# First block's residual halves in the flush of the last attention turn, second stage's weight splits between the first units

## The reference, cut to what matters

```
amp = sigmoid(x @ amp_w + amp_b)
ph = tanh(x @ ph_w + ph_b) * pi
h = (cos(ph) + sin(ph)) * amp
for l in range(2):
    e = h @ ent_w[l] + ent_b[l]
    ent = e @ ent_pw[l] + ent_pb[l]
    h = layer_norm(h + ent, ln3_g[l], ln3_b[l])
    t = einsum('bsd,pdf->pbsf', h, path_w[l]) + path_b[l]
    mod = cos(phase[l]) + sin(phase[l])
    interf = sum(t * mod, over p)
    h = layer_norm(h + interf, ln4_g[l], ln4_b[l])
x = layernorm(x + h)
```

## Time and profile before

| | |
|---|---|
| median of 3 timed runs | 918.68 us (916.01 to 918.86) |
| the profiled execution's own time | 914.03 us |
| its span in the profile | 912.2 us |
| TensorE busy | 858.6 us, 94% |
| VectorE, ScalarE, GpSimd busy | 677.0, 547.0, 491.7 us |
| mean granted clock of TensorE | 0.99 of full |

### The profile page before, as it was taken

How to read it: one execution, slowest core, us unless ns; L and a number is a source line. 1 busy time by engine, 2 the same in 40 slices (tenths; PEclk the granted TensorE clock), 3 DMA queues, 4 the chain that set the end, 5 groups by cost and what they waited for, 6 DMA issues and landing times.

```text
span 912.2 us, 19433 instructions
## 1 busy us (share of the span) xinstructions
PE 858.6 (94%) x5812; PEld 715.1 (78%) x5812; DVE 677.0 (74%) x2061; ACT 547.0 (60%) x1665; POOL 491.7 (54%) x792
## 2 busy tenths in 40 slices
PE   5899999999898999999999999898999999999993
PEld 5778888888787788888888887777778778877773
DVE  4688888888886977777887877758874675666556
ACT  5665556655774666565856566656745645564563
POOL 5456654664665745554645431227760781583387
PEclk9999999999999999999999999999999999999997
DMA  5654434434484956584664638624002002001001
GB/s 183 212 186 148 136 135 168 155 129 152 160 230 139 270 160 199 162 261 115 197 177 154 192 100 266 213 104 162 1 24 70 1 1 92 1 1 45 2 1 47
DMA packets 78939, 117.49 MB, mean 129 GB/s; under 512 B 7888, under 2 KB 41736, under 8 KB 78216
## 3 DMA queue, kind: packets, MB, share of 16 engines
q1 hardware_dynamic: 75416, 112.81, 39.4%
q10 hardware_dynamic: 3440, 3.67, 1.3%
HBM read 58.25 MB, written 17.31 MB: 83 GB/s over the span
## 4 chain that ended last, share of the span: by engine, by line
PE 58%; DVE 6%; SPq 2%; issue 2%; POOL 2%; DMA 2%; ACT 1%; POOLq 0%; DVEq 0%; ACTq 0%
PE bank L161 44%; PE bank L1473 4%; PE bank L1998 3%; PE bank L1496 2%; PE bank L1459 2%; SPq L691 1%; PE bank L1500 1%; DVE stats L1900 1%; DMA xres<-in_x 1%; DVE w_ffn L1685 1%; ACT prob L1079 1%; POOL hT L1793 1%; PE bank L1408 1%; DMA fd<-raw 1%; DVE y L1914 1%
## 5 line engine op out<-in xcount | busy, mean ns | idle before, releaser
L1079 ACT ACTIVATE prob<-bank,nmax 128x128 f32<-128x128 f32 (+1 forms) x512 | 209.2, 432 | 32.8 <-DVE nmax L1224 30.1
L161 PE MATMUL bank<-w_ffn,hT 128*128 128x512 f32 x768 | 188.5, 396 | 1.1 <-DVE w_ffn L1685 0.9
L1224 DVE CUSTOM_DVE_ANT_0 bank<-bank,mask 128x128 f32<-128x128 f32 (+1 forms) x512 | 167.7, 384 | 3.0 <-DVE cv L1172 2.3
L161 PEld LDWEIGHTS bank<-w_ffn,hT 128*128 128x128 f32 x768 | 140.3, 188 | 29.8 <-POOL hT L1793 1.3
L903 POOL TENSOR_TENSOR zone<-raw,zone 128x256 fp32r<-128x256 f32 x128 | 96.2, 783 | 59.7 <-ACT zone L1034 59.7
L1473 PE MATMUL bank<-ident,prob 128*128 128x128 f32 x768 | 119.0, 278 | 1.2 <-ACT probT L1092 1.0
L1092 ACT ACTIVATE probT<-bank 128x512 f32<-128x512 f32 x97 | 58.4, 603 | 95.6 <-PE bank L1500 95.5
L161 PE MATMUL bank<-xT,w_q 128*128 128x256 f32 x768 | 101.9, 284 | 10.5 <-DVE o L1245 9.4
L1079 ACT ACTIVATION_READ_ACCUMULATOR prob<-bank,nmax 128x1 f32 x512 | 111.2, 217 | 0.0
L161 PEld LDWEIGHTS bank<-xT,w_q 128*128 128x128 f32 x768 | 97.8, 190 | 16.0 <-issue 6.0
L161 PE MATMUL bank<-zone 128*128 128x512 f32 x384 | 101.0, 400 | 3.5 <-DVE xT L1147 3.3
(11 more groups left out here) (131 smaller groups left out, 1512.4 us busy)
## 6 DMA issues: line engine op xcount, KB each, us to landing
q<-stage SPq DMA_DIRECT2D x192, 128.0 KB, 2.5
k<-kstage SPq DMA_DIRECT2D x48, 256.0 KB, 4.2
x<-xres SPq DMA_DIRECT2D x16, 512.0 KB, 4.6
raw<-in_ent_wT SPq DMA_DIRECT2D x32, 256.0 KB, 4.1
raw<-in_ent_pw SPq DMA_DIRECT2D x32, 256.0 KB, 4.5
raw<-in_path_w SPq DMA_DIRECT2D x8, 512.0 KB, 3.5
xres<-in_x SPq DMA_DIRECT2D x8, 512.0 KB, 3.8
x1b<-x SPq DMA_DIRECT2D x8, 512.0 KB, 5.0
```

The lines of the kernel that those rows point to most:

```text
L161: ins = t.matmul(out, lhs(a, k), rhs(b, k), start=first and n == 0 and m == 0, stop=last and n == len(kts) - 1 and m == 2, skip_group_chec ...
L1079: ins = s.activation(prob[:, u, c * width:(c + 1) * width], banks[u][:, c * width:(c + 1) * width], ACT.Exp, scale=-1.0, bias=nmax[:, i % ...
L1224: ins = v.tensor_tensor_reduce(scored, scored, mask[:, S - width:S], scale=-1.0, scalar=3e38, op0=ALU.add, op1=ALU.min, accum_out=nmax[:, ...
```

## The change

Three edits. The eight residual halves of block 0 leave GpSimd's entry of the feed-forward and go to its queue in `flush`, four in each step, ahead of `rstd_of`; the wait before them is now for the reader of the first phase gate (`("ph", 0)` drained), since the transposes that read `xb0` precede that gate on TensorE. `residual` becomes a method of `FeedForward`. And VectorE's pieces of stages 1 to 3 are placed anew: pieces 4 and 5 before unit 0, 6 and 7 behind units 0 and 1, and 8 to 15 behind units 4 to 11 where they stood behind units 3 to 10.

```
--- before.py
+++ after.py
@@ -930,6 +930,13 @@
                         path()
                     if i == 0 and t.after == "self":
                         split_x()
+                    if t is flush and i == 0:
+                        g.wait_ge(ffn.s_ln, 32)
+                        g.wait_ge(ffn.s_xb0, 16)
+                        pr.wait_drained(g, last_cross, ("ph", 0))
+                    if t is flush:
+                        for n in range(i * BT, (i + 1) * BT):
+                            ffn.residual(g, 0, *divmod(n, 2))
                     for name in t.fillers(i):
                         if name[0] in ("wo", "wout"):
                             rstd_of(name)
@@ -1601,6 +1608,7 @@
         self.s_c = sem("s3_const")
         self.s_xb0 = sem("s3_x2")
         self.s_xb = [sem("s3_xb0"), sem("s3_xb1")]
+        self.s_res = sem("s3_res")
         self.s_u, self.s_sin = sem("s3_u"), sem("s3_sin")
         self.s_h0 = sem("s3_h0")
         self.s_h0hi, self.s_h0lo = sem("s3_h0hi"), sem("s3_h0lo")
@@ -1609,6 +1617,11 @@
         g.memset(self.ones[:, :], 1.0).then_inc(self.s_c, 1)
         g.memset(self.angles[:, 0:1], PI / 2).then_inc(self.s_c, 1)
         g.memset(self.angles[:, 1:2], -0.25).then_inc(self.s_c, 1)
+
+    def residual(self, g, b, i, half):
+
+        at = slice(half * D // 2, (half + 1) * D // 2)
+        g.tensor_tensor(self.xb[b % 2][:, i, at], self.xb[b % 2][:, i, at], self.lnb[:, at], ALU.add).then_inc(self.s_res, 1)
 
     def load_stage(self, q, n):
         q.dma_start(self.stage_raw[n][:, :, :], self.A["fd"][n // 2, n % 2][:, 0:KT, :]).then_inc(self.s_wraw[n], 16)
@@ -1699,7 +1712,7 @@
     s_bn, s_agg, s_var, s_rstd = sem("s3_bn"), sem("s3_agg"), sem("s3_var"), sem("s3_rstd")
     s_norm = sem("s3_norm")
     s_hhi, s_hlo = sem("s3_hhi"), sem("s3_hlo")
-    s_res = sem("s3_res")
+    s_res = ffn.s_res
     s_cen, s_sum, s_shift, s_scaled = sem("s3_cen"), sem("s3_sum"), sem("s3_shift"), sem("s3_scaled")
     s_fin = sem("s3_fin")
     s_out = sem("s3_out")
@@ -1766,17 +1779,7 @@
                     own = stage_raw[2 * l + 1][:, c, c * P:(c + 1) * P]
                     g.tensor_tensor(own, own, ident[:, :], ALU.add).then_inc(s_id, 1)
 
-            def residual(b, i, half):
-
-                at = slice(half * D // 2, (half + 1) * D // 2)
-                g.tensor_tensor(xb[b % 2][:, i, at], xb[b % 2][:, i, at], lnb[:, at], ALU.add).then_inc(s_res, 1)
-
             residual_of_path(0)
-            g.wait_ge(s_ln, 32)
-            g.wait_ge(ffn.s_xb0, 16)
-            g.wait_ge(s_h0lo, 1)
-            for n in range(2 * BT):
-                residual(0, *divmod(n, 2))
 
             def body(b, plan, last):
                 def rstd_of(u):
@@ -1808,7 +1811,7 @@
                         lo(n - 2)
                     rstd_of(u)
                     if b > 0 and BT < n <= 3 * BT:
-                        residual(b, *divmod(n - BT - 1, 2))
+                        ffn.residual(g, b, *divmod(n - BT - 1, 2))
                     if last and UN - BT <= u < UN - BT + BY_GPSIMD:
                         if u == UN - BT:
                             lo(u - 1)
@@ -1889,7 +1892,8 @@
                 k.wait_drained(("amp", m))
                 ffn.h0(v, m, block * KT + (m + 1))
 
-            ffn.stage_lo(v, 1)
+            for c in range(KT // 2):
+                ffn.piece_lo(v, KT + c)
             v.wait_ge(s_pbias, 16 * NL)
 
             def body(b, plan, last):
@@ -1949,8 +1953,10 @@
                 for kind, n in ffn_order(last):
                     if kind == "mm":
                         unit(n)
-                        if b == 0 and 3 <= n <= 2 * KT + 2:
-                            ffn.piece_lo(v, 2 * KT + n - 3)
+                        if b == 0 and n < KT // 2:
+                            ffn.piece_lo(v, KT + KT // 2 + n)
+                        if b == 0 and KT <= n < 3 * KT:
+                            ffn.piece_lo(v, KT + n)
                         if not last and 2 <= n < 2 + BT // 2:
                             for i in (2 * n - 4, 2 * n - 3):
                                 x2T_lo(k, i, b * BT + (i + 1))
```

2 lines of the change are left out of this document (1 added, 1 removed).

## The result

The changed kernel takes 931.29 us (median of 4 runs, 922.66 to 932.03) against 918.77 us before (4 runs, 916.01 to 921.10): 1.3% slower, ratio 1.0133 with a 95% interval of 1.0106 to 1.0160. The forecast was 926.3 us with a range of 920.8 to 929.8. The direction and the three waits came as forecast; the loss is 12.5 us where 7.6 were said.

A forecast was written before the change was run, and what follows sets the result against it. The prediction took TensorE, busy 94% of 912.2 us, to bound the kernel. Unit 3's transposes +0.75, two waits +6.04 and clock +0.8 gave +7.6 us on 918.68: 926.3 us, range 920.8 to 929.8.

The forecast's parts named there:

- the three waits: New TensorE waits in block 0's feed-forward: 4.4 us for the low half of `hT`, 3.02 us each before units 8 and 12.
- piece 7 ends: VectorE's last second-stage weight subtraction, behind unit 1's statistics: ends at 629.0, holding the fourth stage's weight load 2.25 us later.
- transposes of unit 3, against before: TensorE in block 0's feed-forward: start at 642.25 against 641.51, +0.75 us, bounds -3.7 and +2.3.
- waits before units 8 and 12: TensorE waits for VectorE's pieces 11 and 15, put one unit later: 3.02 us each, 6.04 together.
- clock: TensorE's granted clock falling in the new waits: 1.5 us per fall, 0.8 us taken over all, bounds 0 and 4.5.
- Part one: Eight residual halves move from GpSimd's feed-forward entry to idle time in the flush: cost 0, TensorE starts 1.07 us sooner.
- B: The two waits before units 8 and 12 come, the late load does not: +2.3 us, 921.0 to 922.5; chance 0.10.
- C: Faster: early relief carries through, TensorE's waits before units 8 and 12 are short; all of it 915.0 us; chance 0.04.
- E: Moved halves hold GpSimd's split behind them and the output projection; with 2 us more, 928.3 us; chance 0.04.
- Part two: Pieces 6 and 7 behind units 0 and 1: 2.5 us gained early, then a late load; +0.75 us at unit 3's transposes.
- Part three: Pieces 8 to 15 one unit later: TensorE waits 3.02 us before units 8 and 12 each, 6.04 us together.
- rival D: Several clock falls, work at the low level making new ones: three at 1.5 us, +11.3 us, 930 us; chance 0.09.

The follow-up runs named there:

- e4: The changed kernel with products added on TensorE ahead of the three waits, their result overwritten: 923.73 us, ratio 1.0075 to the kernel before.
- e3: The changed kernel with pieces 8 to 15 behind units 3 to 10 again: 919.24 us, ratio 1.0035 to the kernel before.
- e6: The changed kernel with pieces 6 and 7 both behind unit 0 and 8 to 15 behind units 3 to 10: 916.58 us, ratio 1.0012.
- e5: e3 with GpSimd's identity additions to the fourth stage's weight two units later: 913.31 us, ratio 0.9975 to the kernel before.
- e2: The kernel before with only VectorE's pieces placed as in the changed kernel, halves at GpSimd's entry: 931.01 us, ratio 1.0155.
- e7: The changed kernel with pieces 4 to 7 all ahead of unit 0: 920.91 us, ratio 1.0098 to the kernel before.

## Why the prediction was wrong

Counted from the last gate products, in us, the prediction's steps and what the changed kernel's profile has:

| step | forecast | measured |
|---|---|---|
| first `w_ffn` product | 6.02 | 6.02 |
| unit 0's addition | 11.1 | 11.12 |
| transposes of unit 0 | 14.8 | 14.82 |
| piece 7 ends | 16.2 | 16.28 |
| low half of `hT` done | 24.5 | 24.16 |
| TensorE's wait for it | 4.4 | 4.07 |
| transposes of unit 3, against before | +0.75 | +3.19, with fillers +1.33 |
| waits before units 8 and 12 | 3.02 each | 3.00 each |
| clock | 0.8 (bounds 0 and 4.5) | 6.11 (up to 6.5) |
| sum | 7.6 | 13.87 in the profile, 12.5 timed |

The loss was 6.3 us more than the sum in the profile: 5.3 of it is the clock, 0.6 the norm of unit 2, and 0.4 is the rest that e4 leaves open.

Part one was right, down to the cover that hides the halves; rivals B, C and E did not come. Part two had the mechanism and its size; its last step was 0.6 us short, for I gave unit 2's norm about 0.6 us and it took 1.49 beside GpSimd's low half (the row at 641.99, and 1.49 in e3, e4 and e6 too). Part three was right.

The step that failed is the clock's: "If 3 us of work fall on the lower level, half of it is lost, 1.5 us, once per fall; some of it lies in other waits. I take 0.8 us over all". It was mis-sized twice. The larger part is the count: a fall came in three waits of three, 4.5 us at the forecast's own price, where the sum had about half a fall. I leaned on the one row of 3.32 us that had kept its clock. The other part is the price: the falls cost 2.0 us in the mean and up to 2.9, since after the third the clock stayed low for more than 3 us of work. Comparing the transposes in the changed kernel with those of e4: 31.91 - 30.05 = 1.86 us at the first wait; (663.15 - 655.42) - (657.96 - 651.43) = 1.20 at the second; 1.20 again at the third, and (685.75 - 680.79) - (677.49 - 674.26) = 1.73 in the next unit, 2.93 together, 5.99 over the three falls. It was rival D, given 0.09, that came true, and even its bound of 4.5 us was low; new falls made by work at the low level, which D also named, are not in the profile, where each of the three stands at one of the forecast waits.

The kernel before could have warned of both parts. The slice of 0.83 in the earlier trace rows is only the edge of a fall, with three slices at 0.50 right behind it, and there is a second fall, at a wait of 2.68 us that ends at 28.10 and that the prediction does not name (both windows from the kernel before):

```profile
250.00:253.00 3.00, 3.00 (x25) 2.35 (x18) 2.83 (x15) 1.10 (x4) 2.16 (x4) 0.50 0.75 232
26.00:32.00 6.00, 3.90 (x22) 3.90 (x22) 2.77 (x12) 3.44 (x17) 2.42 (x4) 0.72 0.76 264
```

The Trainium skill states that the throttled level is the default and activity lifts it ("TensorE: Matmul & The Clock Gate", Part 1: The HAM clock gate). The changed kernel's trace agrees: three falls in three waits, none in e4, where fillers kept TensorE at work. The kernel before has the counterexample that I leaned on, 3.32 us at a granted 1.00.

That the timed loss is 12.5 and not 13.87 us fits too: one of the four timed runs took 922.66 us at a mean granted clock of 0.988, the three others 930.83 to 932.03 at 0.978 to 0.981. The first is about what e4 takes. Not settled: what decides in a given run whether a wait of 3 us costs a fall of 1.2 or of 2.9 us; no run here controls that. The profile's further 4.17 us ahead of the flush come from no edit: in the nine profiles the reader of the first phase gate starts between 594.83 and 599.04 us, and in e6, which has the halves in the flush too, at 595.49; the code up to there is the same in all. The clock is a likely cause. In the changed kernel's profile it was low for about 6.8 us behind the wait that ends at 29.86 (3.4 us in the kernel before, at 28.10), and it fell behind the 1.89 us wait that ends at 52.55, where the same wait in the kernel before, at 49.97, kept 1.00:

```profile
28.00:37.00 9.00, 7.14 (x48) 6.24 (x48) 4.91 (x21) 3.97 (x18) 2.58 (x5) 0.62 0.70 217
52.00:56.00 4.00, 3.45 (x16) 3.45 (x17) 3.44 (x13) 3.45 (x17) 3.40 (x8) 0.57 0.81 261
```

By an estimate from these windows that is at most 3.5 of the 4.17 us; no run tests it.

## What to carry to other kernels

A wait of the tensor engine costs its length and then the low clock behind it; price each new wait of 3 us with a whole fall from the start (here 1.2 to 2.9 us), and look for all of them together. When work is moved one unit later in an in-order queue, look for who counts it: here a margin of 0.4 us stood ahead of a step of 3.3 us. A load that is issued behind moved work is late for whoever stands in line at it, and moving that wait back in its own queue (e5) is cheaper than hurrying the load (e6).

## What the runs showed of the hardware

- Behind waits of 4.07, 3.00 and 3.00 us the granted clock averaged 0.57 over 8 us, 0.58 over 4 us and 0.51 over 7 us, while TensorE worked 73 to 89% of that time. I had expected about 3 us of low clock. In the profiles of the changed kernel, e2, e3 and e7 all nine waits of 3.00 to 4.09 us in the feed-forward were followed by a fall.
- The same wait does not always cost a fall. Near 570 us every profile has one of 2.2 us, in code that no run changed: in e2, e3 and e4 the clock fell behind it (e3: 0.50 from 568 to 571 us), in the other six it stayed at 1.00. Only repeated profiles show this.
- 40 products of 128x512 that compute nothing of use made the changed kernel faster, by 4.6 us net (12.5 less 7.9 us over the kernel before); the clock kept its level through the waits, at 1.00 in the three windows of e4.
- A residual half of 128x256 took 0.82 us on GpSimd in a run of four without VectorE's subtractions beside it, and 1.10 us beside them; VectorE's 128x512 subtractions took 1.03 us on average beside the halves (4.11 us for four). With the halves gone they took 0.75, the first of them still beside the identity additions, and 0.65 in the pair at 625.91, where GpSimd was idle.
